# Attention stage: score products in 64x64 tiles, last normalisation on VectorE, weighted products on both sides of the transposes

## The chip, the cores and the metric

The kernel runs on one core of a Trainium2 chip, in float32 throughout the part that is changed. The metric is the device time of one execution in microseconds (us), lower is better. Engines are named as the profile names them: PE is TensorE's matmul stream and PEld its weight loads, DVE is VectorE, ACT is ScalarE, POOL is GpSimd, SP is SyncE, which starts most DMAs.

## The reference

The reference runs two blocks of a modulated transformer on x of 8 batches, 1024 tokens and 128 channels. The first block has a recurrent mixer and a routed expert layer, the second a three-layer linear attention and a position-routed tile layer. The change touches only the linear attention, which is this (16 heads of 8 channels, 8 features a head):

```python
for l in range(3):
    q, k, v = (out @ W[l] + b[l] for W, b in ((Wq, bq), (Wk, bk), (Wv, bv)))   # split in heads
    Qf, Kf = favor(q, omega[l]), favor(k, omega[l])      # exp(u - h), exp(-u - h), scaled
    # for each head, token by token: S += Kf v^T; z += Kf; a = Qf S / (Qf z + 1e-6)
    a = causal_linear_attention(Qf, Kf, v)
    h = layer_norm(out + a @ Wo[l] + bo[l], ln1_g[l], ln1_b[l])
    y = relu(h @ W1[l] + bf1[l]) @ W2[l] + bf2[l]
    out = layer_norm(h + y, ln2_g[l], ln2_b[l])
```

## The kernel before

The program is a row of stages: `setup`, `mixer`, `experts`, `attention`, `tiles`. In `attention` (L1164) the tokens are handled in groups of G = 512 (four chunks of 128). Two independent strands s = 0 and 1, each with its own tiles and its own four PSUM banks (`bank(s, 0)` to `bank(s, 3)`), take turns: strand 0 goes through the first four batches and strand 1 through the last four, 8 groups each, three layers a group. That makes 48 units (group, layer, strand). `slots` (L1251) puts them in a row on every engine: in one slot `a` is the unit whose attention is computed, `f` is the unit before it (the other strand), whose output product, two normalisations and feed-forward part are computed, and `then` is the unit after it, of the same strand as `f`. So each unit spends one slot as `a` and the next as `f`. A hardware loop runs over six slots at a time (three layers, two strands), seven times; the first slots and the last two stand outside it.

Nothing plans the order: each engine has its own `slot` function, its instructions run in the order in which they are written, and semaphores tie the engines together (`wait_ge` waits, `then_inc` signals). What matters here is the end of a slot and the start of the next.

The attention of a group is computed in 16 sub-blocks g of 32 tokens. Within a sub-block, query features and key features are multiplied for all heads together. `kb` (L1326) holds the key features four times over, each time masked to the heads of one residue b (rows p with p // 8 % 4 == b). `qa` (L1425) holds the query features four times, each time masked to one row quarter a (32 rows). So in `qa[:, g, a, :]` only rows 32a to 32a+31 are not zero. `scores` (L1538) multiplies them, per sub-block one call with 128 rows, 128 stationary columns (b, i') and 128 moving columns (a, i); the eight calls of one half of the sub-blocks fill two PSUM banks (`pair`), with column order (j, a, i). `scores(s, n, 0)` writes banks 2 and 3, `scores(s, n, 1)` writes banks 0 and 1. Every float32 matmul call shows in the trace as two passes, each with a weight load.

VectorE multiplies each half by the causal mask into `weights` (L1357, two instructions of 1024 elements a partition, one for each half; `weight_ready` counts them). `carried` (L1545) then multiplies the query features by the running state of all earlier tokens: 32 calls of 64 rows, 64 columns and 36 moving columns, which overwrite banks 2 and 3; therefore it waits for the first mask. `weighed` (L1553) adds the products inside a sub-block: 64 calls with 128 rows, 32 columns, 36 moving columns.

The end of one slot and the start of the next, on TensorE (`slot`, L1568):

- last feed-forward product of `f` (L1616), which VectorE adds to the residual (L1351); then its statistics (L359, L362)
- `scores` 0 and 1 of `a` (L1541)
- wait for the state and for the first mask, `carried` (L1550)
- `transposed_input(then)`: four transposes (L1527) of `xn`, the normalised output of `f`, which is the input of `then`. ScalarE brings it from PSUM to `xT` (L1398)
- `weighed` 0, wait for the second mask, `weighed` 1 (L1557)
- next slot: key and value products from `xT` (L1572, L1573), then the output product of what was `a` and is now `f` (L1564), in two halves that wait for VectorE's division and transposition of the attention result (L1304 to L1308, once for each half of the sub-blocks), then L1578 and on.

The last normalisation of `f` goes this way: statistics on VectorE (`res_stats`); on GpSimd a negated mean (L1476), the variance plus eps (L368), its power -1/2 (L369) and the product of the two (L1478), which is `shift`; then `res_rstd`; then on ScalarE four instructions (L1435), x times rstd plus shift, into `xn` (layers 0 and 1) or into `outcome` (layer 2, the result, which GpSimd gates and adds to x). In the slots where `f` is at layer 2 (two of six), `then` starts at layer 0 with new tokens: its `xn` is made on VectorE by `mod_normalise` (L375), written after the two masks. VectorE's order at the end of a slot is: add and statistics of `f`, mask 0, mask 1, `mod_normalise` if there is one; the next slot begins with the division of half 0 (L1304).

Of the kernel before, what the change touches and what calls it, by code (L numbers as in the profile page):

```python
# [19 lines left out]
ALU = mybir.AluOpType  # L20
ACT = mybir.ActivationFunctionType
AX = mybir.AxisListType.X

P = 128
# [3 lines left out]
GC = 4  # L28
G = GC * P
# [9 lines left out]
L, HEADS, DH, M = 3, 16, 8, 8  # L39
ATTN_EPS = 1e-6  # L40
HQ = 4
SUB = 32
NSUB = G // SUB
# [114 lines left out]
def cst(k, name):  # L158
    return k.const[:, slice(*CONST[name])]
# [1004 lines left out]
def attention(nc, k):  # L1164
# [9 lines left out]
    with ExitStack() as ctx:  # L1174
# [13 lines left out]
        qa = each("qa", [P, NSUB, HQ, SUB])  # L1188
        kb = each("kb", [P, NSUB, HQ, SUB])
        vb = each("vb", [P, NSUB, HQ, HQ, DV])  # L1190
        weights = each("weights", [P, NSUB, HQ, SUB])
        state = each("state", [P, GW, SLOT])
        stats = each("stats", [P, GC, 6])
        mv = each("mv", [P, GC, 2])
        rstd = each("rstd", [P, GC])
        shift = each("shift", [P, GC])
        xmv = each("xmv", [P, GC, 2])
        xrstd = each("xrstd", [P, GC])
        den = each("den", [P, NSUB, HQ])
# [83 lines left out]
        with nc.Block() as block:  # L1283
            @block.vector
            def _(dve):
# [10 lines left out]
                def slot(a, f, then=None):  # L1296
# [49 lines left out]
                    if f:  # L1346

                        s, n = f.s, f.count
                        dve.wait_ge(hres_ready, n + 1)
                        dve.wait_ge(ff_ready, n + 1)  # L1350
                        st.done(nc.vector.tensor_tensor(flat(res[s][:]), bank(s, 1), flat(hres[s][:]), ALU.add))  # L1351
                        statistics(nc, lambda c: res[s][:, c, :], stats[s], mv[s]).then_inc(res_stats, 1)
                    if a:
                        s, n = a.s, a.count
                        for i in two:
                            dve.wait_ge(score_ready, n * 2 + i + 1)
                            nc.vector.tensor_tensor(weights[s][:, 8 * i:8 * i + 8, :, :].rearrange("p j a i -> p (j a) i"),  # L1357
                                                    pair(s, 1 - i).rearrange("p (g i) -> p g i", i=SUB),
                                                    cst(k, "causal").unsqueeze(1).to_broadcast([P, 8 * HQ, SUB]), ALU.mult).then_inc(weight_ready, 1)
                    if then and f and f.l == L - 1:  # L1360
                        mod_normalise(then)

                def cleared(s):

# [26 lines left out]
            def _(act):  # L1391
                def slot(a, f, then):
# [29 lines left out]
                    if a:  # L1422
# [7 lines left out]
                    if f:  # L1430

                        to, ready = (xn, xn_ready) if f.l < L - 1 else (outcome, last_ready)
                        act.wait_ge(res_rstd, f.count * 2 + 2)
                        for c in range(GC):
                            last = nc.scalar.activation(to[f.s][:, c, :], res[f.s][:, c, :], ACT.Identity, bias=shift[f.s][:, c:c + 1], scale=rstd[f.s][:, c:c + 1])  # L1435
                        last.then_inc(ready, 1)

                act.wait_ge(wu_ready, 1)
                nc.scalar.activation(wT[:, 0:2 * L * D], k.psum[:, 0:2 * L * D], ACT.Copy).then_inc(wu_taken, 1)
# [10 lines left out]
            def _(pool):  # L1450
# [6 lines left out]
                def slot(a, f, then=None):  # L1457
# [42 lines left out]
            def _(pe):  # L1500
# [29 lines left out]
                def sums(s, c):  # L1530
# [4 lines left out]
                                      v1[s][quad(j), c, :, r, :], start=True, stop=True)  # L1535
                    return last

                def scores(s, n, i):  # L1538

                    for j in range(8):  # L1540
                        last = mm(pair(s, 1 - i)[:, j * P:(j + 1) * P], kb[s][:, 8 * i + j, :, :].rearrange("p b i -> p (b i)"), qa[s][:, 8 * i + j, :, :].rearrange("p a i -> p (a i)"),  # L1541
                                  start=True, stop=True)
                    last.then_inc(score_ready, 1)

                def carried(s):  # L1545

                    for g in range(NSUB):
                        for h in two:
                            pair_of = slice(h * P // 2, (h + 1) * P // 2)
                            mm(bank(s, 2 + g // 8)[pair_of, g % 8 * GW:(g % 8 + 1) * GW], qa[s][pair_of, g, 2 * h:2 * h + 2, :].rearrange("p a i -> p (a i)"),  # L1550
                               state[s][pair_of, :, g], start=(g % 8 == 0), stop=False, skip_group_check=True)

                def weighed(s, i):  # L1553

                    for g in range(8 * i, 8 * i + 8):
                        for a in range(HQ):
                            last = mm(bank(s, 2 + i)[quad(a), g % 8 * GW:(g % 8 + 1) * GW], weights[s][:, g, a, :],  # L1557
                                      vb[s][:, g, a, :, :].rearrange("p b e -> p (b e)"), start=False, stop=True, skip_group_check=True)
                    last.then_inc(out_ready, 1)

# [7 lines left out]
                def slot(a, f, then):  # L1568
# [43 lines left out]
                    if f:  # L1612
# [28 lines left out]


VEC_STEPS = 2 * L * (6 + 1 + 1)
POOL_STEPS = 2 * (1 + L * (1 + 1 + 1 + 3) + 2)


def tiles(nc, k, ins, out):
# [296 lines left out]
```

## Time and profile before

| what | us |
|---|---|
| median of 3 runs (lowest, highest) | 2099.49 (2096.52, 2099.62) |
| profiled execution, its own time | 2101.77 |
| its span, first to last instruction | 2099.7 |
| PE busy | 1749.7 (83%) |
| DVE busy | 1510.0 (72%) |
| ACT busy | 961.7 (46%) |
| POOL busy | 999.5 (48%) |

Busy shares are over the whole span. In the page's row of forty slices TensorE is at nine tenths or more in nearly all of the attention stage, and the granted TensorE clock is at nine tenths or more in most of its slices. Line numbers are those of the kernel before. In a timeline row the first number is the start of a run of like instructions in us from the start of the span, the second the time from its first start to its last end, the number behind x how many they are; since matmuls are pipelined, the time that one row takes from the engine is the distance to the start of the next row. A releaser in brackets is what ended an idle time.

### The profile page before, as it was taken

How to read it: one execution, taken by the hardware profiler on the slowest of the kernel's cores; microseconds unless marked ns; L12 is line 12 of the kernel's file. 1: busy time of each engine (PE TensorE's matmuls, PEld its weight loads, DVE VectorE, ACT ScalarE, POOL GpSimd, SP SyncE). 2: the span in 40 equal slices, each digit the busy share in tenths (PEclk: the TensorE clock that was granted, in tenths of full speed). 3: DMA queues.
4: the chain of work that ended last, by engine and by line, in shares of the span. 5: the costliest groups of instructions: out<-in, count | busy, mean ns of one | idle time of the engine just before them, and what ended most of it. 6: DMA issues, size and time to landing. Idle time of an engine off the chain costs nothing. (4 is left out here: it accounts for less than half of the span.)

```text
span 2099.7 us, 60516 instructions
## 1 busy us (share of the span) xinstructions
PE 1749.7 (83%) x23836; PEld 1333.8 (64%) x23837; DVE 1510.0 (72%) x3643; ACT 961.7 (46%) x1834; POOL 999.5 (48%) x1141
## 2 busy tenths in 40 slices
PE   5655554379928999999999999999999999996898
PEld 4333344279926777767767767767767767774798
DVE  2899964459867777767778768768768768774765
ACT  2555555456614454445444444444444444442331
POOL 0677747769843334324324324334325324333797
PEclk8877765589969999999999999999999999997799
DMA  7400011122220000000000000000000000000011
GB/s 202 79 0 0 0 28 33 41 62 63 64 94 2 2 2 2 2 3 2 2 3 2 2 3 2 2 3 2 2 3 2 2 3 2 2 2 1 11 35 36
DMA packets 60699, 42.41 MB, mean 20 GB/s; under 512 B 19721, under 2 KB 54801, under 8 KB 59953
## 3 DMA queue, kind: packets, MB, share of 16 engines
q1 hardware_dynamic: 47504, 25.35, 4.7%
q0 software_dynamic: 4352, 8.99, 1.3%
q10 hardware_dynamic: 8608, 4.67, 0.8%
q8 instruction: 181, 2.97, 0.6%
q14 instruction: 54, 0.43, 0.1%
HBM read 24.22 MB, written 14.77 MB: 19 GB/s over the span
## 5 line engine op out<-in xcount | busy, mean ns | idle before, releaser
L1476 POOL TENSOR_TENSOR at_shift<-at_mv,const 128x4 f32<-128x4 f32 x48 | 9.7, 202 | 376.4 <-DVE at_mv L362 376.4
L1541 PE MATMUL psum<-at_qa,at_kb 128*128 128x128 f32 x1536 | 181.9, 277 | 4.2 <-DVE at_state L1338 4.2
L1616 PE MATMUL psum<-attn_w,at_qa 128*128 128x128 f32 x1536 | 184.1, 278 | 0.0
L1608 PE MATMUL psum<-at_vT,attn_w 128*128 128x512 f32 x384 | 180.6, 613 | 0.9 <-ACT at_vT L1417 0.9
L1541 PEld LDWEIGHTS psum<-at_qa,at_kb 128*128 128x128 f32 x1536 | 177.8, 194 | 4.3 <-DVE at_state L1338 4.3
L1616 PEld LDWEIGHTS psum<-attn_w,at_qa 128*128 128x128 f32 x1536 | 175.2, 192 | 2.8 <-issue 0.7
L1421 ACT ACTIVATE at_qa<-psum,attn_bf 128x512 f32<-128x512 f32 x192 | 132.0, 687 | 91.3 <-PE psum L1608 91.3
L1326 DVE TENSOR_SCALAR at_kb<-at_kf,const 128x512 f32<-128x512 f32 x192 | 158.9, 887 | 0.0
L1332 DVE STREAM_TRANSPOSE at_vb<-at_vT 32x512 uint32<-32x512 uint32 x192 | 134.7, 702 | 1.9
L1841 PE MATMUL psum<-tilesT,ti_masked 128*128 128x128 f32 x1024 | 120.0, 279 | 13.2 <-POOL ti_masked L1803 13.2
L1357 DVE TENSOR_TENSOR at_weights<-psum,const 128x1024 f32<-128x1024 f32 x96 | 116.3, 1211 | 18.5 <-PE psum L1541 17.0
L1841 PEld LDWEIGHTS psum<-tilesT,ti_masked 128*128 128x128 f32 x1024 | 117.8, 195 | 15.0 <-issue 15.0
L368 POOL TENSOR_TENSOR at_rstd<-at_mv,const 128x4 f32<-128x4 f32 x96 | 19.4, 202 | 222.0 <-DVE at_mv L362 222.0
L1425 ACT ACTIVATE at_qa<-at_qf,const 128x512 f32<-128x512 f32 x192 | 122.3, 710 | 0.0
L1435 ACT ACTIVATE at_xn<-at_kt,at_shift,at_rstd 128x128 f32<-128x128 f32 x128 | 52.8, 483 | 148.4 <-POOL at_shift L1478 148.4
L1608 PEld LDWEIGHTS psum<-at_vT,attn_w 128*128 128x128 f32 x384 | 70.0, 192 | 74.0 <-issue 70.6
L1550 PE MATMUL psum<-at_state,at_qa 64*64 64x36 f32 x3072 | 111.7, 243 | 0.4
L1550 PEld LDWEIGHTS psum<-at_state,at_qa 64*64 64x64 f32 x3072 | 104.5, 142 | 6.4 <-issue 1.5
L1534 PEld LDWEIGHTS psum<-at_v,at_kt 32*32 32x32 f32 x6144 | 62.4, 103 | 68.9 <-issue 68.1
L375 DVE TENSOR_SCALAR at_sqk<-at_kt,at_mv,at_rstd 128x128 f32<-128x128 f32 x192 | 53.5, 343 | 67.8 <-POOL at_rstd L369 67.8
L369 POOL TENSOR_TENSOR at_rstd<-at_rstd,const 128x4 f32<-128x4 f32 x96 | 97.5, 1015 | 7.5
L655 PE MATMUL psum<-const,mx_xn 128*128 128x128 f32 x72 | 20.1, 434 | 89.7 <-ACT mx_xn L558 89.7
(305 smaller groups left out, 4442.9 us busy)
## 6 DMA issues: line engine op xcount, KB each, us to landing
ex_xs<-sorted_x SPq DMA_DIRECT2D x80, 65.0 KB
x<-in_L_attn_x ACTq DMA_DIRECT2D x8, 512.0 KB, 7.6
ex_feats<-token_y SPq DMA_DIRECT2D x4, 1024.0 KB, 7.8
out<-x SPq DMA_DIRECT2D x16, 256.0 KB, 2.3
expert_w<-in_L_ffn_w SPq DMA_DIRECT2D x1, 2048.0 KB, 8.8
attn_w<-in_L_attn_W SPq DMA_DIRECT2D x2, 768.0 KB
token_y<-ex_y,ex_place POOLq DMA_INDIRECT x72
sorted_x<-ex_spare SPq DMA_DIRECT2D x1, 1040.0 KB, 7.8
```

What stands on the lines that cost most here:

```text
L369: return nc.gpsimd.tensor_tensor(rstd[:], rstd[:], cst(k, "minus_half")[:, 0:n], ALU.pow)
L1326: last = nc.vector.tensor_scalar(kb[s][:, :, b, :], kf[s][:].rearrange("p (j i) -> p j i", i=SUB), cst(k, "mask_b")[:, b:b + 1], None, ALU ...
L1332: last = nc.vector.transpose(vb[s][q, :, :, b, 0:DH].bitcast(U32), vT[s][q, :].bitcast(U32).rearrange("p (j a d) -> p j a d", a=HQ, d=DH))
L1357: nc.vector.tensor_tensor(weights[s][:, 8 * i:8 * i + 8, :, :].rearrange("p j a i -> p (j a) i"), pair(s, 1 - i).rearrange("p (g i) -> p g ...
L1421: nc.scalar.activation(hidden[f.s][:, t, :], bank(f.s, t), ACT.Relu, bias=k.bf1[:, f.l, t:t + 1]).then_inc(hid_taken, 1)
L1425: last = nc.scalar.activation(qa[s][:, :, i, :], qf[s][:].rearrange("p (j i) -> p j i", i=SUB), ACT.Copy, scale=cst(k, "mask_a")[:, i:i + 1])
L1534: last = mm(bank(s, j)[quad(r), c * GW:(c + 1) * GW], kt[s][quad(j), c, quad(r)], v1[s][quad(j), c, :, r, :], start=True, stop=True)
L1541: last = mm(pair(s, 1 - i)[:, j * P:(j + 1) * P], kb[s][:, 8 * i + j, :, :].rearrange("p b i -> p (b i)"), qa[s][:, 8 * i + j, :, :].rearr ...
L1550: mm(bank(s, 2 + g // 8)[pair_of, g % 8 * GW:(g % 8 + 1) * GW], qa[s][pair_of, g, 2 * h:2 * h + 2, :].rearrange("p a i -> p (a i)"), state ...
L1608: mm(bank(f.s, c), k.w1[:, f.l, c * P:(c + 1) * P], hT[f.s][:], start=True, stop=True).then_inc(hid_ready, 1)
L1616: last = mm(bank(f.s, 1)[:, c * D:(c + 1) * D], hidden[f.s][:, t, c * P:(c + 1) * P], k.w2[:, f.l, t, :], start=(t == 0 and c == 0), stop= ...
L1841: last = nc.tensor.matmul(bank(s, B)[:, c * D:(c + 1) * D], masked[s][:, t, c * P:(c + 1) * P], k.tilesT[:, t, :], start=(t == 0), stop=(t ...
```

## The change

Scores: each 128x128 call becomes four calls of 64 rows by 64 columns by 64 moving columns, for row half h (rows 64h to 64h+63, which are the query quarters a = 2h and 2h+1) and column half e (key copies b = 2e and 2e+1). The result of row half h goes to the h-th of the two banks of the pair, so a bank belongs to one row half; column half e goes to partitions 64e to 64e+63. What is left out are only products with the zero rows of `qa`. The layout of `weights` follows (half i, row half h, sub-block j, a, i). Calls of the scores go from 16 to 64 a slot.

Normalisation: the last normalisation of `f` leaves ScalarE and becomes four VectorE instructions (`normalise`, L372, as already used for `hn`), between mask 0 and mask 1; `mod_normalise(then)` also stands between the masks now, ahead of it. GpSimd no longer computes `shift` (two instructions fewer, L1476 and L1478).

TensorE's order at the end of a slot: `carried`, `weighed` 0, the transposes of `then`, wait for the second mask, `weighed` 1. A second wait on `cols_scaled`, which is long fulfilled, stands ahead of the scores.

```diff
-        weights = each("weights", [P, NSUB, HQ, SUB])
+        weights = each("weights", [P, 2, 2, 8, 2, SUB])
...
+                    def causal(i):
+                        dve.wait_ge(score_ready, a.count * 2 + i + 1)
+                        nc.vector.tensor_tensor(weights[a.s][:, i, :, :, :, :].rearrange("p h j a i -> p (h j a) i"),
+                                                pair(a.s, 1 - i).rearrange("p (g i) -> p g i", i=SUB),
+                                                cst(k, "causal").unsqueeze(1).to_broadcast([P, 8 * HQ, SUB]), ALU.mult).then_inc(weight_ready, 1)
                     if a:
-                        s, n = a.s, a.count
-                        for i in two:
-                            dve.wait_ge(score_ready, n * 2 + i + 1)
-                            nc.vector.tensor_tensor(weights[s][:, 8 * i:8 * i + 8, :, :].rearrange("p j a i -> p (j a) i"),
...
+                        causal(0)
                     if then and f and f.l == L - 1:
                         mod_normalise(then)
+                    if f:
+                        to, ready = (xn, xn_ready) if f.l < L - 1 else (outcome, last_ready)
+                        dve.wait_ge(res_rstd, f.count * 2 + 2)
+                        normalise(nc, lambda c: res[f.s][:, c, :], mv[f.s], rstd[f.s], to[f.s]).then_inc(ready, 1)
+                    if a:
+                        causal(1)
...
-                        act.wait_ge(res_rstd, f.count * 2 + 2)
-                        for c in range(GC):
-                            last = nc.scalar.activation(to[f.s][:, c, :], res[f.s][:, c, :], ACT.Identity, bias=shift[f.s][:, c:c + 1], scale=rstd[f.s][:, c:c + 1])
-                        last.then_inc(ready, 1)
...
-                        st.mark(nc.gpsimd.tensor_tensor(shift[s][:], mv[s][:, :, 0], cst(k, "minus_one")[:, 0:GC], ALU.mult))
-                        st.done(inverse_deviation(nc, st, k, rstd[s], mv[s]))
-                        nc.gpsimd.tensor_tensor(shift[s][:], shift[s][:], rstd[s][:], ALU.mult).then_inc(res_rstd, 1)
+                        inverse_deviation(nc, st, k, rstd[s], mv[s]).then_inc(res_rstd, 1)
...
                     for j in range(8):
-                        last = mm(pair(s, 1 - i)[:, j * P:(j + 1) * P], kb[s][:, 8 * i + j, :, :].rearrange("p b i -> p (b i)"), qa[s][:, 8 * i + j, :, :].rearrange("p a i -> p (a i)"),
-                                  start=True, stop=True)
+                        g = 8 * i + j
+                        for h in two:
+                            for e in two:
+                                last = mm(pair(s, 1 - i)[half_of(e), h * G + j * P // 2:h * G + (j + 1) * P // 2],
+                                          kb[s][half_of(h), g, 2 * e:2 * e + 2, :].rearrange("p b i -> p (b i)"),
+                                          qa[s][half_of(h), g, 2 * h:2 * h + 2, :].rearrange("p a i -> p (a i)"), start=True, stop=True)
...
+                        pe.wait_ge(cols_scaled, 1)
                         pe.wait_ge(sum_taken, n + 1)
...
                         carried(s)
+                        pe.wait_ge(vb_ready, n + 1)
+                        weighed(s, 0)
                         if then:
                             transposed_input(then)
-                        pe.wait_ge(vb_ready, n + 1)
-                        weighed(s, 0)
                         pe.wait_ge(weight_ready, n * 2 + 2)
                         weighed(s, 1)
```

## Rows read from the trace of the kernel before

**Rows 1.** Windows view: busy us (and instructions) of each engine, granted clock, DMA
```profile
780.00:1900.00 1120.00, 1067.84 (x18032) 786.16 (x18032) 833.43 (x1957) 539.32 (x924) 400.74 (x486) 0.99 0.01 2
```
**Rows 2.** Timeline of TensorE, end of one slot and start of the next
```profile
1041.96 3.74 PE L1541 MATMUL psum<-at_qa,at_kb 128*128 128x128 f32 x32
1045.62 2.33 PE L1550 MATMUL psum<-at_state,at_qa 64*64 64x36 f32 x64
1047.88 0.66 PE L1527 MATMUL psum<-const,at_xn 128*128 128x128 f32 x4
1048.47 1.33 PE L1557 MATMUL psum<-at_vb,at_weights 128*32 128x36 f32 x128
1049.73 1.12 PE L1572 MATMUL psum<-at_xT,attn_w 128*128 128x512 f32 x2
...
1051.55 1.41 PE L1564 MATMUL psum<-attn_w,at_sqq 128*128 128x128 f32 x8
1052.80 1.02 PE L1578 MATMUL psum<-at_xT,omega 128*128 128x512 f32 x2
...
1067.68 0.72 PE L1541 MATMUL psum<-at_qa,at_kb 128*128 128x128 f32 x5
```
**Rows 3.** Timeline of VectorE in the same slot
```profile
1042.23 0.69 DVE L1351 TENSOR_TENSOR at_kt<-psum,at_xn 128x512 f32<-128x512 f32 x1 [1.03 <-PE psum L1616]
...
1043.90 0.38 DVE L362 BATCH_NORM_AGGREGATE at_mv<-at_stats 128x2 f32<-128x6 f32 x4
1044.20 1.19 DVE L1357 TENSOR_TENSOR at_weights<-psum,const 128x1024 f32<-128x1024 f32 x1
1045.73 1.23 DVE L1357 TENSOR_TENSOR at_weights<-psum,const 128x1024 f32<-128x1024 f32 x1 [0.34 <-PE psum L1541]
1049.28 0.19 DVE L1304 TENSOR_SCALAR at_den<-psum 128x32 f32<-128x32 f32 x1 [2.32 <-PE psum L1557]
...
1051.75 0.45 DVE L1308 STREAM_TRANSPOSE at_sqq<-at_kf 128x256 uint32<-128x256 uint32 x1
```
**Rows 4.** Timeline of ScalarE and of GpSimd in the same slot, one answer each
```profile
1046.13 1.65 ACT L1435 ACTIVATE at_xn<-at_kt,at_shift,at_rstd 128x128 f32<-128x128 f32 x4 [4.63 <-POOL at_shift L1478]
1048.58 0.78 ACT L1398 ACTIVATE at_xT<-psum,attn_cols 128x512 f32<-128x512 f32 x1 [0.80 <-PE psum L1527]
...
1044.36 0.20 POOL L1476 TENSOR_TENSOR at_shift<-at_mv,const 128x4 f32<-128x4 f32 x1 [9.68 <-DVE at_mv L362]
...
1044.79 1.02 POOL L369 TENSOR_TENSOR at_rstd<-at_rstd,const 128x4 f32<-128x4 f32 x1
```
**Rows 5.** Groups by line, 780 to 1900 us: count, busy us, mean ns, idle before
```profile
L1550 PE MATMUL psum<-at_state,at_qa 64*64 64x36 f32 x2688 | 97.7, 243 | 0.4
L1534 PE MATMUL psum<-at_v,at_kt 32*32 32x36 f32 x5376 | 64.0, 204 | 18.8 <-ACT at_qf L1414 18.8
L1557 PE MATMUL psum<-at_vb,at_weights 128*32 128x36 f32 x5376 | 58.9, 201 | 6.8 <-issue 6.8
```
**Rows 6.** Timelines of TensorE and VectorE, a slot where the first mask is late
```profile
1150.54 3.74 PE L1541 MATMUL psum<-at_qa,at_kb 128*128 128x128 f32 x32
1154.33 1.89 PE L1550 MATMUL psum<-at_state,at_qa 64*64 64x36 f32 x51
...
1152.96 2.58 DVE L1357 TENSOR_TENSOR at_weights<-psum,const 128x1024 f32<-128x1024 f32 x2
```
**Rows 7.** Timelines of VectorE and TensorE, a slot with new tokens
```profile
1129.58 1.11 DVE L375 TENSOR_SCALAR at_xn<-x,at_xmv,at_xrstd 128x128 f32 x4
...
1130.75 0.66 PE L1527 MATMUL psum<-const,at_xn 128*128 128x128 f32 x4
```
**Rows 8.** Windows view, one hold and one fall of the clock
```profile
55.70:59.10 3.40, 1.83 (x5) 0.52 (x3) 0.17 (x2) 3.37 (x5) 1.96 (x6) 1.00 0.76 95
59.10:62.50 3.40, 0.00 (x0) 0.00 (x0) 3.36 (x4) 3.37 (x6) 0.00 (x0) 1.00 0.11 2
...
912.50:915.91 3.41, 1.26 (x129) 1.15 (x128) 2.46 (x8) 1.03 (x2) 1.86 (x2) 1.00 0.05 12
915.91:919.32 3.41, 1.70 (x2) 0.83 (x3) 0.25 (x1) 0.00 (x0) 0.00 (x0) 0.50 0.02 5
```

More of the change, by code:

```diff
@@ L1195, in attention @@
         rstd = each("rstd", [P, GC])
-        shift = each("shift", [P, GC])
         xmv = each("xmv", [P, GC, 2])
@@ L1352, in slot @@
                         statistics(nc, lambda c: res[s][:, c, :], stats[s], mv[s]).then_inc(res_stats, 1)
-                    if a:
-                        s, n = a.s, a.count
-                        for i in two:
-                            dve.wait_ge(score_ready, n * 2 + i + 1)
-                            nc.vector.tensor_tensor(weights[s][:, 8 * i:8 * i + 8, :, :].rearrange("p j a i -> p (j a) i"),
-                                                    pair(s, 1 - i).rearrange("p (g i) -> p g i", i=SUB),
-                                                    cst(k, "causal").unsqueeze(1).to_broadcast([P, 8 * HQ, SUB]), ALU.mult).then_inc(weight_ready, 1)
+                    def causal(i):
[3 more added lines that the diff above has]
+                                                cst(k, "causal").unsqueeze(1).to_broadcast([P, 8 * HQ, SUB]), ALU.mult).then_inc(weight_ready, 1)
+                    if a:
+                        causal(0)
                     if then and f and f.l == L - 1:
                         mod_normalise(then)
+                    if f:
[4 more added lines that the diff above has]
+                        causal(1)
                 def cleared(s):
@@ L1429, in slot @@
                         nc.scalar.activation(carry[l][s][:], state[s][:, :, NSUB], ACT.Copy)
-                    if f:
-                        to, ready = (xn, xn_ready) if f.l < L - 1 else (outcome, last_ready)
-                        act.wait_ge(res_rstd, f.count * 2 + 2)
-                        for c in range(GC):
-                            last = nc.scalar.activation(to[f.s][:, c, :], res[f.s][:, c, :], ACT.Identity, bias=shift[f.s][:, c:c + 1], scale=rstd[f.s][:, c:c + 1])
-                        last.then_inc(ready, 1)
                 act.wait_ge(wu_ready, 1)
@@ L1536, in sums @@
                     return last
+                half_of = lambda h: slice(h * P // 2, (h + 1) * P // 2)
                 def scores(s, n, i):
                     for j in range(8):
-                        last = mm(pair(s, 1 - i)[:, j * P:(j + 1) * P], kb[s][:, 8 * i + j, :, :].rearrange("p b i -> p (b i)"), qa[s][:, 8 * i + j, :, :].rearrange("p a i -> p (a i)"),
-                                  start=True, stop=True)
+                        g = 8 * i + j
[4 more added lines that the diff above has]
+                                          qa[s][half_of(h), g, 2 * h:2 * h + 2, :].rearrange("p a i -> p (a i)"), start=True, stop=True)
                     last.then_inc(score_ready, 1)
@@ L1548, in carried @@
                         for h in two:
-                            pair_of = slice(h * P // 2, (h + 1) * P // 2)
-                            mm(bank(s, 2 + g // 8)[pair_of, g % 8 * GW:(g % 8 + 1) * GW], qa[s][pair_of, g, 2 * h:2 * h + 2, :].rearrange("p a i -> p (a i)"),
-                               state[s][pair_of, :, g], start=(g % 8 == 0), stop=False, skip_group_check=True)
+                            mm(bank(s, 2 + g // 8)[half_of(h), g % 8 * GW:(g % 8 + 1) * GW], qa[s][half_of(h), g, 2 * h:2 * h + 2, :].rearrange("p a i -> p (a i)"),
+                               state[s][half_of(h), :, g], start=(g % 8 == 0), stop=False, skip_group_check=True)
                 def weighed(s, i):
@@ L1556, in weighed @@
                         for a in range(HQ):
-                            last = mm(bank(s, 2 + i)[quad(a), g % 8 * GW:(g % 8 + 1) * GW], weights[s][:, g, a, :],
+                            last = mm(bank(s, 2 + i)[quad(a), g % 8 * GW:(g % 8 + 1) * GW], weights[s][:, i, a // 2, g % 8, a % 2, :],
                                       vb[s][:, g, a, :, :].rearrange("p b e -> p (b e)"), start=False, stop=True, skip_group_check=True)
@@ L1643 @@
 VEC_STEPS = 2 * L * (6 + 1 + 1)
-POOL_STEPS = 2 * (1 + L * (1 + 1 + 1 + 3) + 2)
+POOL_STEPS = 2 * (1 + L * (1 + 1 + 1 + 1) + 2)
 def tiles(nc, k, ins, out):
```

## The prediction

> **What bounds the kernel now.** I read the windows view of the attention stage first. TensorE is busy 1067.84 of 1120 us (95%), VectorE 833 (74%), ScalarE 539, GpSimd 401, at a mean granted clock of 0.99 [rows 1]. So TensorE's order decides, and the question is which other engine ends its waits once one part of it gets shorter. For that I read the end of a slot in the timelines, engine beside engine. Times below count from the first score product, 1041.96 in that slot; the next slot's is 1067.68, so a slot takes 25.72 us [rows 2].
>
> - TensorE: scores 0 to 3.66, carried 3.66 to 5.92 (2.26), transposes to 6.51 (0.59), weighed products to 7.77 (1.26), key and value products (L1572, L1573) 1.82 to 9.59, output product L1564 1.25 to 10.84, where L1578 starts [rows 2].
> - VectorE: it can start the residual add at 0.27, because the feed-forward product has just ended; statistics end at 2.32; mask 0 runs 2.24 to 3.43, mask 1 3.77 to 5.00; then it idles 2.32 until the weighed products come; the division and transposition of both halves run from 7.32 to 10.24 (2.92) [rows 3].
> - GpSimd 2.40 to 4.1, ScalarE's normalisation 4.17 to 5.82, its copy to xT 6.62 to 7.40 [rows 4].
>
> So three things nearly coincide: mask 0 (3.43) ends just before the scores (3.66), the normalised input (5.82) just before carried ends (5.92), and xT (7.40) just before the weighed products end (7.77).
>
> **Part 1, scores.** There are 32 passes now in 3.66 us, 114 ns each. After the change there are 128 passes of 64 columns. If all four quarters of the array work at once, four passes take the time of half a pass: 32 x 57 = 1.83 us. If the two row halves cannot work at once, it is twice that, 3.66. The nearest row for two row halves at work by turns is carried, 2688 passes in 97.7 us, 36 ns each, for only 36 columns [rows 5]; 128 of them are 4.65 us unscaled, and by columns (64/36) 8.3. The nearest rows for quarters at work together are the weighed products, 5376 passes in 58.9 us, 11 ns, and the sums (L1534), which put each row quarter in a bank of its own, 64.0 us for 5376, 12 ns [rows 5]; scaled by 64/36 that is 2.5 to 2.7. Carried writes both row halves into one bank and runs 3 times slower a pass than the two others; the new scores keep the banks of the row halves apart. I take 1.9 us, with 1.83 and 4.65 as ends and 8.3 as remote.
>
> The Trainium skill says in "TensorEngine Tiling (Array Packing)", Restrictions and Gotchas, that different row tiles cannot access the same PSUM bank at once. The pace of carried agrees with that, and by that rule the new scores would overlap in full. The same page (Tiling Modes, Key Properties) says that a change of tiling mode drains the engine; this speaks against the split in part 3, and the trace has only whole steps for it, so its cost stands there by rows.
>
> Of the 1.7 us that the scores save, nearly nothing reaches the path. Carried overwrites the banks that mask 0 reads. Mask 0 is behind the residual add and the statistics on VectorE, all of which start when the feed-forward product ends, and that moves nowhere: it still ends at 3.43. In the slot in which the mask ends late (1152.96 and half of 2.58, so 1154.2), carried starts 1154.33, about 0.15 later, and after the scores [rows 6]. So carried starts at 3.58, not 3.66: 0.08 saved in five slots of six, nothing in the sixth, where VectorE is already the later one. TensorE gets a new idle time of about 1.6 us a slot. Part 1 is worth 0.07 us a slot.
>
> **Part 2, normalisation.** Without L1476 and L1478 (0.20 each) the power L369 starts at about 2.7 and ends at 3.70 [rows 4]. VectorE, free at 3.43, waits until 3.75 and needs 1.12 (four instructions; 1.11 for the same form in rows 7). xn is ready at 4.9 instead of 5.82. Mask 1 moves from 3.77 to 4.9 and ends at 6.1; weighed 1, which waits for it, is due at 7.1. In two slots of six both normalisations stand between the masks: mask 1 ends at 3.43 + 1.11 + 1.12 + 1.2 + small gaps = 6.95, with the latency 7.1, just in time. There the transposes now wait for VectorE (its end 1130.69, their start 1130.75, 0.15 later than in the plain slot) [rows 7]; this wait goes. VectorE gains 1.12 us of work a slot, inside its 2.32 of idle time before L1304; ScalarE and GpSimd get lighter, which frees nothing, since both wait for others. The earlier xn is hidden: after part 3 the transposes are due only at 6.5. Worth 0 in plain slots, up to 0.15 in two of six.
>
> **Part 3, order.** Carried 3.58 to 5.84. Weighed 0 takes half of 1.26 plus a second fill and switch, for which I put 0.04 (no row has it; at worst as much as carried's 36-column start, 0.2, at best nothing): to 6.51. Transposes 0.59, to 7.10, weighed 1 0.67, to 7.77: here as before. But the copy to xT starts 0.70 after the first transpose and takes 0.78 [rows 2, 4]: 6.51 + 1.48 = 7.99, and with about 0.11 until the first product (xn's end 5.82 to the transposes' start 5.92 is no more than that) L1572 starts at 8.10, 0.33 later than before. In return the division of half 0 starts after weighed 0: that ended 0.81 before L1304 if counted from the first weighed product (6.51 to 7.32, with half of the calls in it) [rows 2, 3], so now at 5.84 + 0.81 = 6.65, and both halves are through at 9.57 instead of 10.24. L1564, due at 8.10 + 1.82 = 9.92, then waits for nothing: 8 x 0.11 = 0.89 instead of 1.25, a gain of 0.36. L1578 starts at 10.81 instead of 10.84.
>
> **Sum.** In a plain slot 0.03 us is gained; in the slot of the late mask about 0.07 is lost (0.08 less from part 1); in the two with new tokens between 0.1 lost and 0.15 gained, the copy to xT being the bound there as well. From L1578 to the next scores every step is TensorE's own, or the one wait for the query features (18.8 us in 42 slots, 0.45 each [rows 5]), which the change doesn't touch. Over six slots this is a gain of 0 to 0.3, and over 48 slots 0 to 2.5. A little more may come from TensorE's fetch waits, 6.8 us at L1557 [rows 5], some of which may fall into the new idle time; 20% more TensorE instructions in a slot may as well add one. I take -2.5 us on the profiled execution: 2101.8 - 2.5 = 2099.3. That execution lies 2.07 above its span (2099.7) and 2.3 above the median, so the forecast for a median is 2097, within 0.2% (4.2 us, about what can be told apart here).
>
> **Rivals.**
> - *The clock falls in the new idle time.* The new gap is 1.6 to 1.75 us, twice to three times anything regular in this stage. In one stretch of 3.40 us with 1.83 busy the clock stayed at 1.0, in one with 1.26 of 3.41 busy it was 0.50 (the level of 1.2 GHz) right after [rows 8]. A stretch with the gap and carried beside it has some 1.7 busy, and carried fills only half of the array. For: it lies between the two. Against: the scores and products on both sides are dense. Price: if in every second slot 3.4 us run at half speed, 24 x 1.7 = 41 us, so 2140; in every slot 2180. It decides from about one slot in ten (8 us) on. This is the case on the other side.
> - *The row halves don't overlap in spite of their banks.* At carried's 36 ns the scores end at 4.65, carried starts at 4.8, 1.1 later than before: 48 x 1.0 = 48, 2147; at exactly two at once (3.66) only 0.1 a slot, 2102. Against it are the sums at 12 ns.
> - *The chain at xT is shorter than I have it.* If the copy starts earlier, or TensorE's order lets the transposes slip, L1572 starts at the 7.77 of TensorE's own work and the full 0.36 of L1564 is kept, or half of it: 48 x 0.18 to 0.36 = 9 to 17 us, with some fetch waits absorbed 2082 to 2090. For: the order puts each wait on an earlier signal; against: rows 4 leave no slack in this copy.
>
> **Chances.** Forecast 0.50, its own range 2091 to 2104 (0.31 of it within 0.2%, 0.16 faster, 0.03 slower by more); clock 0.25; no overlap 0.10; shorter chain 0.15. So faster 0.31, same 0.31, slower 0.38. The range 2084 to 2145 leaves out the end of the faster case and the worse half of the two slow ones.
>
> **What would show it.** L1541: 128 passes a slot in 1.8 to 2.0 us. Then idle time of TensorE at L1550 of 1.4 to 1.7 us, released by VectorE's L1357: that is the step on which the forecast stands, and if it isn't there, the forecast is wrong. L1435 gone, four more L375 between two L1357, POOL without L1476 and L1478. L1572 waiting for ScalarE's L1398 (about 0.3), L1564 at 0.9 us with no wait for L1308. L1578 10.8 after the first score. Granted clock 0.99 for the stage; at 0.95 or less the first rival has come.

## The result, and the profile after

The changed kernel takes 2155.8 us (median of 4 runs, 2145.49 to 2157.71) against 2099.55 for the kernel before (now 4 runs, the profiled one among them); the ratio is 1.0259 with the interval 1.0224 to 1.0294. It is slower by 56 us. The forecast was 2097 and the range ended at 2145, so the time lies outside it. It is the first rival that came, and it cost more than I had made room for. The profiled execution took 2155.13 us with a span of 2153.0, and the comparison below is made on it.

The windows view of the stage comes first again, in the same columns as [rows 1].

```profile
780.00:1900.00 1120.00, 1010.00 (x20960) 726.80 (x20956) 839.18 (x2036) 447.16 (x720) 372.43 (x388) 0.93 0.01 3
```

TensorE is less busy (1010 of 1120 instead of 1068), ran more instructions in the same time (20,960 against 18,032), and its granted clock is 0.93 instead of 0.99, below the 0.95 that was named as the sign of the first rival. Over the whole span it is 0.871 against 0.904. Next is a slot in which nothing disturbs the clock; this is TensorE's timeline, to be read against [rows 2].

```profile
1225.16 2.10 PE L1544 MATMUL psum<-at_qa,at_kb 64*64 64x64 f32 x128
1228.65 2.33 PE L1553 MATMUL psum<-at_state,at_qa 64*64 64x36 f32 x64 [1.39 <-DVE at_weights L1354]
1230.91 0.77 PE L1560 MATMUL psum<-at_vb,at_weights 128*32 128x36 f32 x64
1231.61 0.66 PE L1525 MATMUL psum<-const,at_xn 128*128 128x128 f32 x4
1232.19 0.77 PE L1560 MATMUL psum<-at_vb,at_weights 128*32 128x36 f32 x64
1233.13 1.12 PE L1575 MATMUL psum<-at_xT,attn_w 128*128 128x512 f32 x2 [0.17 <-ACT at_xT L1405]
1234.10 1.02 PE L1576 MATMUL psum<-at_xT,attn_wv 128*128 128x512 f32 x2
1234.95 1.05 PE L1567 MATMUL psum<-attn_w,at_sqq 128*128 128x128 f32 x8
1235.84 1.02 PE L1581 MATMUL psum<-at_xT,omega 128*128 128x512 f32 x2
```

This is the slot of the forecast. Carried (L1553) starts 3.49 after the first score (forecast 3.58), after an idle time that VectorE's mask ended. Before, TensorE idled 0.4 us in all ahead of carried [rows 5]; now this is its largest wait in the stage (780 to 1900 us: total, times, longest):

```profile
PE psum L1553 <- DVE at_weights L1354: 50.8, 40, 1.8
```

L1567, the output product, takes 0.89 without its wait. L1581, which was L1578, starts at 10.68 (forecast 10.81, before 10.84). From the first score to the next it is 25.66 us (the next score starts at 1250.82), against 25.72 before. VectorE in the same slot, against [rows 3]:

```profile
1227.01 0.38 DVE L362 BATCH_NORM_AGGREGATE at_mv<-at_stats 128x2 f32<-128x6 f32 x4
1227.31 1.19 DVE L1354 TENSOR_TENSOR at_weights<-psum,const 128x1024 f32<-128x1024 f32 x1
1228.80 1.12 DVE L375 TENSOR_SCALAR at_xn<-at_kt,at_mv,at_rstd 128x128 f32<-128x128 f32 x4 [0.30 <-POOL at_rstd L369]
1229.84 1.22 DVE L1354 TENSOR_TENSOR at_weights<-psum,const 128x1024 f32<-128x1024 f32 x1
1231.72 0.19 DVE L1303 TENSOR_SCALAR at_den<-psum 128x32 f32<-128x32 f32 x1 [0.67 <-PE psum L1560]
```

The mask is still where it was, behind the statistics; the normalisation stands between the masks. Only 14 of 40 slots away from the ends of the hardware loop keep the full clock as this one does. In the timeline of TensorE in another slot the clock falls between the scores and carried, and the windows view of that stretch shows it (the 1.00, 0.50 and 1.00 near the end of each row are the clock):

```profile
1114.67 2.09 PE L1544 MATMUL psum<-at_qa,at_kb 64*64 64x64 f32 x128
1118.56 2.91 PE L1553 MATMUL psum<-at_state,at_qa 64*64 64x36 f32 x64 [1.79 <-DVE at_weights L1354]
1121.40 1.19 PE L1560 MATMUL psum<-at_vb,at_weights 128*32 128x36 f32 x64
1122.51 1.12 PE L1525 MATMUL psum<-const,at_xn 128*128 128x128 f32 x4
1123.56 1.19 PE L1560 MATMUL psum<-at_vb,at_weights 128*32 128x36 f32 x64
1124.75 2.00 PE L1575 MATMUL psum<-at_xT,attn_w 128*128 128x512 f32 x2
1126.58 1.02 PE L1576 MATMUL psum<-at_xT,attn_wv 128*128 128x512 f32 x2
```

```profile
1116.30:1119.71 3.41, 1.62 (x69) 1.51 (x61) 3.12 (x13) 0.00 (x0) 1.24 (x2) 1.00 0.01 2
1119.71:1126.54 6.83, 6.83 (x170) 5.25 (x166) 4.71 (x12) 1.02 (x2) 5.33 (x5) 0.50 0.02 5
1126.54:1129.95 3.41, 3.41 (x15) 2.03 (x14) 1.31 (x5) 1.37 (x2) 0.99 (x1) 1.00 0.00 0
```

Carried takes 2.84 instead of 2.26, the transposes 1.05 instead of 0.58, the first key product 1.83 instead of 0.97. The trace also holds the granted clock as a list of stretches, and the falls can be counted in it. Between 650 and 1900 us the clock falls to its lower level (1.2 GHz) 33 times, for 167 us in all; in the kernel before it does so 6 times, for 27 us. Each of those 6 goes with the end of a pass of the hardware loop, where TensorE idles about 3.9 us.

The sum can be made from the slots, counted from one of VectorE's copies of v to the next, 47 in all. The first one, where the clock is low in both kernels, takes 23.37 us against 25.74 before; the kernel with the scores alone (below) shows the same 23.34. Another 6 hold the end of the loop: 33.06 us on average against 31.25 before, together 10.9 more. Of the other 40, 10 have 6.83 us at the lower level and take 28.47, 16 have 3.41 us and take 27.13, and 14 have none and take 26.15; before, all 40 kept the full clock and took 25.99. So 10 x 2.32 + 16 x 0.98 = 39 us go with falls inside the slots and 10.9 with the ends of the loop, where the clock is lower for longer as well (51 us against 27). A further 40 x 0.16 = 6.5 us touch slots at full clock too, and the first slot gives back 2.4. Together that is 54, and the 47 slots differ by 54.1 (1306.7 against 1252.6).

### The profile page after: what moved, and what is told of

Read it like the earlier page. It is cut to its first block and busy times, and to the rows that moved or that the text cites. A ratio compares the mean times of both kernels' runs of the same rounds, so it can differ in the third digit from the quotient of the medians.

```text
span 2153.0 us, 69634 instructions
## 1 busy us (share of the span) xinstructions
PE 1735.0 (81%) x28443; PEld 1304.1 (61%) x28445; DVE 1560.8 (72%) x3835; ACT 882.2 (41%) x1642; POOL 982.9 (46%) x1045
## 5 line engine op out<-in xcount | busy, mean ns | idle before, releaser
L1553 PE MATMUL psum<-at_state,at_qa 64*64 64x36 f32 x3072 | 120.9, 249 | 60.9 <-DVE at_weights L1354 60.8
L1553 PEld LDWEIGHTS psum<-at_state,at_qa 64*64 64x64 f32 x3072 | 114.7, 151 | 66.4 <-issue 66.3
L1405 ACT ACTIVATE at_xT<-psum,attn_cols 128x512 f32<-128x512 f32 x32 | 24.9, 777 | 271.5 <-PE psum L1525 271.5
L1312 DVE TENSOR_TENSOR at_kt<-psum,at_xres 128x512 f32<-128x512 f32 x48 | 33.2, 692 | 120.0 <-PE psum L1567 113.0
L1544 PE MATMUL psum<-at_qa,at_kb 64*64 64x64 f32 x6144 | 104.5, 222 | 9.0 <-issue 5.0
L1544 PEld LDWEIGHTS psum<-at_qa,at_kb 64*64 64x64 f32 x6144 | 96.8, 137 | 15.8 <-issue 10.2
L1560 PE MATMUL psum<-at_vb,at_weights 128*32 128x36 f32 x6144 | 97.9, 229 | 7.4 <-issue 7.3
```

Of the source, the lines that this page charges most:

```text
L1544: last = mm(pair(s, 1 - i)[half_of(e), h * G + j * P // 2:h * G + (j + 1) * P // 2], kb[s][half_of(h), g, 2 * e:2 * e + 2, :].rearrange("p ...
L1553: mm(bank(s, 2 + g // 8)[half_of(h), g % 8 * GW:(g % 8 + 1) * GW], qa[s][half_of(h), g, 2 * h:2 * h + 2, :].rearrange("p a i -> p (a i)"), ...
```

## The experiments

Theory A: the clock falls because TensorE now idles between the scores and carried. Theory B: the time goes into the additional TensorE instructions and changes of tile shape. Theory C: it goes into the new place of the normalisation and the new order. Each kernel was timed together with the kernel before on one chip: 2096.68 us in the first group (six fillers, scores alone, rest alone), 2097.52 on another chip in the second (the other four). Each of these is the median of 13 runs; in the second group 12 of them lie within 1.6 us and one took 2123.05. Between groups, and against the 2155.8 of the changed kernel, the ratios are therefore the better measure. A fall is counted as above, from 650 to 1900 us.

**Fill the gap.** Six products that nobody needs, on the changed kernel:

```diff
                         scores(s, n, 0)
                         scores(s, n, 1)
+                        if f:
+                            for c in range(6):
+                                mm(bank(f.s, 3)[:, c % GC * D:(c % GC + 1) * D], k.w4[:, WQ, l, :], k.w1[:, l, c % GC * P:(c % GC + 1) * P], start=True, stop=True)
```

> The changed kernel with six more 128x128x128 products a slot between the scores and carried, into a bank that nobody reads then (12 passes, about 1.34 us of the 1.6 us gap, so that carried should not start later); their result is not used. Theory A (the clock falls because TensorE idles between the scores and carried): granted clock back to 0.98 or 0.99 in the stage, undisturbed slots stay at 25.65 us, median 2093 to 2104. Theory B (the time went into more TensorE instructions, their fetch, and the two more changes of tile shape): those are all still there, so 2140 or more and the instructions even grow.

Measured: 2113.2 us (2107.61 to 2116.47), ratio 1.007 (1.0048 to 1.0093). Its windows row, and the slowest part of one of its slots on TensorE (L1631 are the fillers):

```profile
780.00:1900.00 1120.00, 1059.77 (x22236) 773.94 (x22232) 861.98 (x2095) 459.40 (x740) 382.65 (x398) 0.98 0.01 3
```

```profile
1208.16 1.74 PE L1544 MATMUL psum<-at_qa,at_kb 64*64 64x64 f32 x103
1210.38 0.62 PE L1544 MATMUL psum<-at_qa,at_kb 64*64 64x64 f32 x25 [0.49 <-issue]
1210.93 1.60 PE L1631 MATMUL psum<-attn_w 128*128 128x128 f32 x12
1212.46 2.33 PE L1553 MATMUL psum<-at_state,at_qa 64*64 64x36 f32 x64
```

More work made the kernel faster: by 43 us from median to median, by 40 us if the ratios are compared (1.0259 and 1.007). The falls are down from 33 to 6, all six at the ends of the loop, so theory A holds for the larger part. But it missed its own range of 2093 to 2104: about 16 us stay. The rows show one place: in the middle of the scores TensorE stops, for nothing that the profile names ("issue").

**The scores alone**, on the kernel before:

```diff
-                        last = mm(pair(s, 1 - i)[:, j * P:(j + 1) * P], kb[s][:, 8 * i + j, :, :]..., qa[s][:, 8 * i + j, :, :]...)
+                        (the loop over h and e of the change, its layout of weights, its wait on cols_scaled)
```

> The kernel before with the 64x64 scores alone (and the layout of the weights that goes with them); normalisation on ScalarE and the order of before. Theory A: the gap is there (scores end at 1.9, carried starts at 3.5 to 3.6), so the clock falls as in the changed kernel: clock of the stage about 0.93, median 2135 to 2165. Theory C (the order of the weighed products and the normalisation cost the time): 2098 to 2105.

Measured: 2131.43 us (2128.82 to 2137.57), ratio 1.0162 (1.0143 to 1.0181), 36 falls. The clock of the stage is 0.93, and TensorE waits for the mask as in the changed kernel:

```profile
780.00:1900.00 1120.00, 1016.99 (x21253) 734.45 (x21248) 800.73 (x1904) 519.53 (x892) 390.48 (x473) 0.93 0.01 3
```

```profile
L1556 PE MATMUL psum<-at_state,at_qa 64*64 64x36 f32 x2607 | 101.9, 248 | 50.9 <-DVE at_weights L1357 50.7
```

So the scores alone bring the falls, with the rest as it was. The time is just below the expected band of 2135 to 2165, and below the changed kernel by 24 us from median to median, 20 us by the ratios.

**The rest alone**, the changed kernel with the 128x128 scores and the layout of `weights` that goes with them:

```diff
-                        for h in two:
-                            for e in two:
-                                last = mm(pair(s, 1 - i)[half_of(e), ...
+                        last = mm(pair(s, 1 - i)[:, j * P:(j + 1) * P], kb[s][:, 8 * i + j, :, :]..., qa[s][:, 8 * i + j, :, :]...)
```

> The changed kernel with the 128x128 scores of before; normalisation between the masks and the split weighed products stay. Theory A: no gap, no falls of the clock, carried at 3.67, L1578's counterpart at about 10.85: median 2096 to 2106. Theory C: 2130 or more.

Measured: 2095.43 us (2091.62 to 2096.88, 10 runs), ratio 0.9993 (0.9984 to 1.0003), 5 falls. The clock is that of the kernel before:

```profile
780.00:1900.00 1120.00, 1070.21 (x18231) 792.19 (x18227) 881.25 (x2141) 469.55 (x756) 391.49 (x407) 0.99 0.01 2
```

The time is 0.6 us under the expected band. Theory C is out as far as normalisation and order stand by themselves: alone they cost nothing and gain nothing that can be measured. Together with the small scores they are not free, as the difference of 20 us above shows.

**Less filler**, two products instead of six (`range(2)`):

> As the first experiment, with two filler products a slot instead of six (4 passes, about 0.45 us), so about 1.1 us of idle time stay between the scores and carried. The result of the fillers is not used. Theory A, with the clock following how long TensorE idles there: fewer falls than in the changed kernel (33 in the stage) or none; with none the median is that of six fillers, 2110 to 2116, with as many as before 2150. If the fillers helped by anything else than TensorE's activity (their number), a third of the gain, about 2142.

Measured: 2120.47 us (2116.81 to 2123.18), ratio 1.0114 (1.0098 to 1.0131). The timeline shows the part of the gap that stays:

```profile
1043.97 2.10 PE L1544 MATMUL psum<-at_qa,at_kb 64*64 64x64 f32 x128
1046.00 0.71 PE L1631 MATMUL psum<-attn_w 128*128 128x128 f32 x4
1047.46 2.33 PE L1553 MATMUL psum<-at_state,at_qa 64*64 64x36 f32 x64 [0.74 <-DVE at_weights L1354]
```

The profile, which counts a matmul to its modelled end, shows 0.74 us idle there instead of the 1.39 of an undisturbed slot of the changed kernel. The clock of the stage is 0.97. There are 17 falls instead of 33; only 7 of the 40 slots away from the ends of the loop have one, against 26, and these take 0.98 us more than the others (27.09 against 26.11). A third of the fillers brought about three quarters of the gain (30 of 40 us by the ratios), so it is not their number that helps, but that TensorE idles for less time.

**Small scores for one half only**, on the changed kernel:

```diff
+                SMALL = (True, False)
                 def scores(s, n, i):
...
+                        if not SMALL[i]:
+                            last = mm(pair(s, 1 - i)[:, j * P:(j + 1) * P], kb[s][:, g, :, :]..., qa[s][:, g, :, :]..., start=True, stop=True)
+                            continue
```

> The changed kernel with 64x64 scores for the first half of the sub-blocks only; the second half is 128x128 as before. Scores end at about 2.8, carried starts at 3.5, so 0.7 us of idle time; 96 instructions a slot more than before instead of 192. Theory A: clock 0.98 or 0.99, no falls but those at the loop's end. Theory F (what is left above 2096 in the kernel with six fillers, 16 us, are waits for instructions, which come in blocks of 256 and 0.9 to 1.4 us each, and for which TensorE waits where it runs through a block faster): half as many or fewer of these waits, so 2096 to 2105. Without theory F (the 16 us belong to the split or the scores' tile shape as such): 2104 or more.

Measured: 2096.01 us (2094.84 to 2100.64, 10 runs), ratio 0.9988 (0.9961 to 1.0014), clock 0.99, 6 falls.

```profile
1039.01 1.16 PE L1553 MATMUL psum<-at_qa,at_kb 64*64 64x64 f32 x64
1040.10 2.05 PE L1548 MATMUL psum<-at_qa,at_kb 128*128 128x128 f32 x16
1042.49 2.33 PE L1562 MATMUL psum<-at_state,at_qa 64*64 64x36 f32 x64 [0.34 <-DVE at_weights L1354]
```

With a short gap (0.34 by the profile) the clock holds without filler. The 16 us above the kernel before are gone too, with half of the additional instructions; this speaks for the waits for instructions. By itself it does not rule out a cost of the tile shape, since that change is halved as well.

These waits can be counted. I took, from 780 to 1900 us, every distance over 0.35 us from the start of one weight load to the start of the next inside the scores, the sums, carried or the weighed products, and looked up the transfer of instructions that ended last before it. The queue of instructions moves blocks of 16 KB, most of them in 0.9 to 1.4 us. In the whole execution there were 181 blocks in the kernel before, 217 after, 221 with six fillers. From 780 to 1900 us there were 152 and 175 in the first two, 23 more for 5852 more instructions of TensorE (the counts in the windows rows, products and weight loads together), so a block is about 256 instructions. The profile's rows of that queue for these three kernels, in this order, and the pauses (the last two kernels are described further down):

```profile
q8 instruction: 181, 2.97, 0.6%
```

```profile
q8 instruction: 217, 3.56, 0.7%
```

```profile
q8 instruction: 221, 3.62, 0.7%
```

| kernel | pauses | us in all |
|---|---|---|
| before | 9 | 8.8 |
| changed | 19 | 16.1 |
| changed, six fillers | 29 | 20.4 |
| scores alone | 8 | 7.3 |
| rest alone | 4 | 2.2 |
| changed, two fillers | 11 | 8.4 |
| one half small | 12 | 7.0 |
| early mask | 40 | 43.6 |
| early mask, one half small | 6 | 3.6 |

Every one of these 138 pauses ends 1.2 to 1.6 us after the end of such a block, while the blocks come 6.1 to 7.4 us apart on average. Between the kernel with six fillers and the one with the rest alone the pauses differ by 18.2 us, and the 40 slots away from the ends of the loop by 16 (26.32 against 25.92 us each). So there the time is TensorE's waits for its own instructions. The ends of the loop are a second part: 32.04 against 30.53 us each, 9 us together, with the clock low for 41.0 us against 20.5. With both, the two profiled executions are 23.1 us apart. The medians differ by 17.8 only; the profiled execution of the kernel with six fillers was its slowest run.

**Use the freed time: early mask.** Scores 0 ahead of the last quarter of the feed-forward product, and VectorE's order mask 0, residual add, statistics, mask 1, normalisation:

```diff
                         for t in range(FT):
+                            if a and t == FT - 1:
+                                (waits for cols_scaled, sum_taken, kb_ready, qa_ready)
+                                scores(a.s, a.count, 0)
...
+                    if a:
+                        causal(0)
                     if f:
                         (residual add, statistics)
+                    if a:
+                        causal(1)
...
                         weighed(s, 0)
-                        if then:
-                            transposed_input(then)
                         pe.wait_ge(weight_ready, n * 2 + 2)
                         weighed(s, 1)
+                        if then:
+                            transposed_input(then)
```

> A version meant to use what the smaller scores free: scores 0 stand ahead of the last quarter of the feed-forward product, mask 0 on VectorE ahead of the residual add, mask 1 in VectorE's wait for the deviation, the weighed products in one piece again and the transposes behind them. Carried then waits for nobody; TensorE idles about 0.5 us ahead of the transposes and 0.9 us behind them instead of 1.6 us at one place. Undisturbed slots 25.2 to 25.5 us. With theory A and F: if the clock holds 2085 to 2105 (the waits for instructions remain), if the two idle times so close to each other make it fall as well 2120 to 2150.

Measured: 2118.82 us (2113.61 to 2128.92), ratio 1.0087 (1.007 to 1.0103), 19 falls: between the two bands. An earlier expectation for this version, written before the first experiments were run, had been 2075 to 2095. TensorE's longest waits in it, from 780 to 1900 us (total, times, longest):

```profile
PE psum L1575 <- ACT at_xT L1405: 33.2, 35, 1.1
PE psum L1560 <- issue: 32.2, 33, 1.9
```

The first is the exposed copy to xT, as counted beforehand (0.9 a slot). The second I had not seen coming in this size: in 33 of 41 slots the weighed products stop, most often for about a microsecond. Where they stop moves on from slot to slot, after 125, 104, 81, 60 and 39 of the 128 passes in consecutive slots, as it should if the stops go with blocks of a fixed number of instructions and not with a place in the program. Carried starts as soon as the scores end, so bursts of small products (the scores, carried, the weighed products) follow each other without the idle time that TensorE had ahead of carried. That this idle time had let the next block arrive was not tested by itself.

**Early mask with one half small.** The previous kernel, with 128x128 products for scores 1 and the transposes between the weighed products as in the change:

```diff
+                SMALL = (True, False)
...
                         weighed(s, 0)
+                        if then:
+                            transposed_input(then)
                         pe.wait_ge(weight_ready, n * 2 + 2)
                         weighed(s, 1)
-                        if then:
-                            transposed_input(then)
```

> The version before this one with 128x128 products for scores 1, and the transposes between the weighed products again: TensorE idles about 0.35 us ahead of the transposes and 0.3 behind weighed 1, and has 96 instructions a slot more than before instead of 192. Theory A and F: clock 0.99, few waits for instructions, slots of 25.1 to 25.4 us, median 2070 to 2088, below both kernels. If VectorE's early mask delays the residual add by more than 0.3 us, it is 2090 to 2100.

Measured: 2085.9 us (2083.92 to 2087.42), ratio 0.9942 (0.9926 to 0.9959), clock of the stage 0.98, 7 falls (six at the ends of the loop, one at the end of the stage). It beats both kernels, the one before by 0.6%. One slot on TensorE:

```profile
1032.65 2.94 PE L1634 MATMUL psum<-attn_w,at_qa 128*128 128x128 f32 x24
1035.53 1.16 PE L1553 MATMUL psum<-at_qa,at_kb 64*64 64x64 f32 x64
1036.62 1.16 PE L1634 MATMUL psum<-attn_w,at_qa 128*128 128x128 f32 x8
1037.61 1.95 PE L1548 MATMUL psum<-at_qa,at_kb 128*128 128x128 f32 x16
1039.49 2.33 PE L1562 MATMUL psum<-at_state,at_qa 64*64 64x36 f32 x64
1041.75 0.77 PE L1569 MATMUL psum<-at_vb,at_weights 128*32 128x36 f32 x64
1042.53 0.66 PE L1525 MATMUL psum<-const,at_xn 128*128 128x128 f32 x4
1043.12 0.77 PE L1569 MATMUL psum<-at_vb,at_weights 128*32 128x36 f32 x64
1044.06 1.13 PE L1584 MATMUL psum<-at_xT,attn_w 128*128 128x512 f32 x2 [0.17 <-ACT at_xT L1405]
...
1057.97 2.94 PE L1634 MATMUL psum<-attn_w,at_qa 128*128 128x128 f32 x24
```

Carried follows the scores without a wait, and this slot takes 25.32 us instead of 25.72. On average the 40 slots away from the ends of the loop take 25.64 instead of 25.99, 14 us together; the medians differ by 11.6. Two things changed from the version before it, and an early mask with 128x128 scores throughout was not run, so the gain is not divided among them.

## Why the prediction was wrong

- **What bounds the kernel: right.** TensorE's order decides, and the first mask takes over as soon as the scores are shorter.
- **Part 1, scores: right.** 128 passes take 2.03 us where the next work follows at once (1043.97 to 1046.00 in the kernel with two fillers), forecast 1.9. That is 16 ns a pass, where one pass of 64 columns alone was put at 57, so row halves and column halves do run together. Carried starts at 3.49, forecast 3.58. "Worth 0.07 us a slot" fits the least disturbed slots of the kernel with the scores alone, 25.67 us against 25.72. In the rival without overlap the sum was loose: carried 1.1 us later in 48 slots is 53 us, not 48.
- **Parts 2 and 3: right.** xn is ready at 4.76 (1229.92), forecast 4.9; L1575 starts at 7.97 behind the copy, forecast 8.10; L1581 at 10.68, forecast 10.81. The kernel with the rest alone, with 128x128 scores, measures no change.
- **The gap and the clock: here it failed.** The step that failed is the cost of the new idle time. "TensorE gets a new idle time of about 1.6 us a slot" stood in the text, but the sum put it at nothing and expected a granted clock of 0.99; the case in which the clock falls got a chance of 0.25. The runs showed 0.93, and 39 us for falls inside the slots. The filler kernel shows the cause directly: the same kernel with the gap closed is 40 us faster, with no fall inside a slot. The argument against the rival, that "the scores and products on both sides are dense", did not carry. The stretch before the fall shown above had 1.62 of 3.41 us busy, between the 1.83 of the stretch that held and the 1.26 of the one that fell in [rows 8]. A nearer stretch of the kernel before had been read and was not weighed; its clock is 1.00, and 0.50 in the stretch after it:

```profile
185.50:188.87 3.37, 1.62 (x13) 1.24 (x11) 3.26 (x5) 1.45 (x3) 1.11 (x1) 1.00 0.00 0
```

  Busy time over such a stretch does not sort the cases either: before the 26 falls inside slots TensorE was busy for 1.6 to 2.7 of 3.41 us, in many of them longer than in the stretch of [rows 8] that held. The rows left the question open, and I decided it for the side that agreed with the rest of the sum.
- **The ends of the loop: left out.** The gap was called "twice to three times anything regular in this stage". But TensorE idles for up to 4.0 us at each end of the loop (6 times, 23.2 us in all, at L1572), and the clock fell there in the kernel before as well. The sum had nothing for a longer low clock at these places; it came to 10.9 us.
- **The price of the falls: near, in part by luck.** I had 41 us for 24 falls of 1.7 us each. There are 26 slots with a fall, 16 at 0.98 us and 10 at 2.32 us, together 39.
- **Fetch waits: too small.** I let them come out even ("some of which may fall into the new idle time; 20% more TensorE instructions in a slot may as well add one"). Measured as in the table, they went up from 8.8 to 16.1 us in the changed kernel, and to 20.4 with the gap filled.

The sum in hindsight, against the kernel before: falls inside slots 39, ends of the loop 11, the first slot -2, and 6.5 in slots at any clock, where the pauses for instructions have grown by 7. That is 54 of the measured 56.

Open: the changed kernel has about as many falls as the scores alone (33 and 36) and is 20 us slower by the ratios. Away from the ends of the loop its 40 slots take 20 us more. 9 us of that are pauses for instructions (16.1 against 7.3). Most of the rest goes with longer falls: with the scores alone 26 slots have 3.41 us at the lower level and 1 has 6.83, in the changed kernel it is 16 and 10, and a long one costs 1.34 us more. Why they are longer is open. An obvious suspect is that the copy to xT is no longer hidden, so that TensorE has a second idle time shortly after the first. The trace speaks against it: in 6 of the 10 long falls, the one shown above among them, the profile has TensorE busy for the whole 6.83 us, and in the other four it idles for 0.14 to 0.45 us of them.

## What to carry to other kernels

Before making one part of a busy engine's work shorter, find what its successor waits for next: here a mask on another engine ended 0.23 us before the work that was halved, so nearly all of the gain turned into idle time. Here this idle time on TensorE was not free: 1.4 to 1.8 us a slot by the profile cost 39 us inside the slots through the clock, 0.74 us some 7 (7 slots at 0.98), 0.34 us nothing. What worked here was to move the successor's cause first (the mask ahead of the residual add) and to shorten only as much as the chain could use (one half of the scores). Count the instructions as well as the time.

## What the runs showed of the hardware

- Useless products made a kernel faster: 12 more passes a slot in an idle time, 2155.8 to 2113.2 us (ratio to the kernel before 1.0259 and 1.007).
- 64x64 tiles with a PSUM bank for each row half worked together: 128 passes of 64 columns in 2.03 us, 16 ns each, against 57 ns for half of a 128-column pass of the kernel before. Carried, whose passes of 36 columns have both row halves in one bank, takes 35 ns each. That the bank is the reason was not tested.
- Bursts of small products can outrun the supply of instructions. The transfer of a block of 16 KB mostly takes 0.9 to 1.4 us, and the pauses end 1.2 to 1.6 us after its end; the weighed products run through 256 instructions in 1.26 us [rows 2], the small scores in 2.03 us. Where such bursts followed each other, TensorE stood: up to 1.9 us at a time, about 1 us a slot in the early-mask kernel.
- A fall of the clock cost less than half of its length: a slot with 3.41 us at the lower level took 0.98 us more than one without, one with 6.83 us took 2.32 us more.
